# Two heads at once in row tiles of the array, compact keys, and new orders of work, in a fused four-layer transformer block

## The chip, the cores and the metric

One core of one Trainium2 chip runs the whole program in one launch. The metric is the device time in microseconds (us); lower is better.

## The reference, cut to what matters

The input is 32 sequences of 256 tokens with 128 features. Each sequence goes through four blocks: attention, feed-forward, rotary causal attention, and a block of two layers of local attention with a gated feed-forward each.

```python
x = x + attention16(layernorm(x))          # 16 heads of 8, scores / sqrt(128), all 256 keys
x = x + relu(layernorm(x) @ w1 + b1) @ w2 + b2           # width 512
x = x + attention16_rope_causal(layernorm(x)) @ wo.T     # 16 heads of 8, rotary, causal mask
x = x + ffn(layernorm(x))                  # two layers, each:
    # q, k, v = shift(x) @ wqkv : 8 heads of 64, l2 norm, rotary with scale
    # softmax(q k) over a window of 64 and the one before it, then @ wo, residual
    # shift, layernorm with gain and bias, @ w1, a * gelu(g), @ w2, residual
```

All of it is float32.

## The kernel before, in words

**Streams and units.** The work on a sequence is cut into four streams: ATTN0 (first attention and first feed-forward), ATTN1 (rotary attention), LOCAL0 and LOCAL1 (the two local layers). A stream is a list of units, each a small job that every engine knows (the unit `maxes` is, for TensorE, a matmul into a PSUM bank, and for VectorE the maximum over that bank). A bank is handed over by two semaphores of its own, one for filled and one for emptied. Every stream has one set of buffers, so it works on one sequence at a time, in order; the four streams work on four or five different sequences at once.

**Orders.** In which order an engine takes the units of the four streams is written out by hand in strings: `TURNS["tensor"]` and so on, one digit for the stream of the next unit, and `BANKS` gives the bank of each unit in TensorE's order. The strings describe one round of 216 units, one sequence of each stream. `plan()` plays the round 37 times: stream k takes up sequence n in round n + `TAKES_UP[k]` (0, 2, 3, 4), and its units from number `BEGINS[k]` on are a round later. So 27 rounds are full (rounds 5 to 31), and the five at either end are the same round with the units left out whose sequence is below 0 or above 31.

**Scores of the 16-head attentions.** A head has 8 features, and to keep float32 accuracy in the faster fp32r matmul each number is split in a high and a low part and the head's maximum is put in too: 32 rows of the contraction for a head, four heads to the 128 rows. `qT` holds four heads' queries on 128 partitions. `kT` before is wide: for each of the 16 heads a 128 x 256 block that is zero outside the head's 32 partitions, so a full-height matmul of `qT` (four heads) and the block gives one head's scores. ScalarE copies the transposed keys to `kS`, and SyncE's queue spreads them by four DMAs (L483) into `kT`; the unit `maxes` waits for them (`k_in`). `maxes` (L971; L975/L976 and L980/L982 with the causal mask as a matmul with the identity) makes 512 columns for a unit: two heads of 256 keys, or four of 128. VectorE takes the maxima (L802). `scores` (L992) makes the transposed scores, two matmuls of 256 queries for each unit; ScalarE takes the exponential (L656), GpSimd zeroes the causal part (L546). `mix` (L1011) multiplies the values with these, four heads at once, each in 32 columns of the array.

**Scores of the local attention.** A head has 64 features, so a pair of heads fills the 128 partitions. `kT2` is wide in the same way: two blocks for each pair, half zero, written by two half-height ACTIVATEs for each unit (L642). `scores2` is a mask matmul (L1071, L1079) and, in plain float32, L1073 or L1080; VectorE takes the maxima (L878), ScalarE the exponentials (L689). A plain float32 matmul is two instructions in the trace, an fp32r one is one. `mix2` (L1103) uses 64 columns of the array for each of two heads.

Of the kernel before, what the change touches and what calls it, by code (L numbers as in the profile page):

```python
# [8 lines left out]
STREAMS = 4  # L9
P = 128  # L10
# [17 lines left out]
def shape_constants():  # L28
# [23 lines left out]
    def table(c, s):  # L52
# [15 lines left out]
TAKES_UP = (0, 2, 3, 4)  # L68
BEGINS = (21, 33, 25, 8)


TURNS = {
    "tensor": (
        "20002220223311111333333222220002222222000022103333"
        "33333211100100333331000001130102222001233303303230"
        "02333331111133122000032220012220222222221111333330"
        "00330011311110011331011013333331112222222110100010"
        "0022200010111103"
    ),
    "scalar": (  # L80
        "22222332111333331312222000000022222222000033333333"
        "31111100000333330000031111222222200000333333222333"
        "33311111112200000002220012222221111333333322222300"
        "00330000033303333331111111111111112222222111122211"
        "1110000000000003"
    ),
    "vector": (
        "20020220232233303333321222222223333222221111133333"
        "32333111110000000000002113200000311130000011002233"
        "33320133302333301133222222213000003202223333220001"  # L90
        "11111222223111111111122133333223330000000000000000"
        "1111111111122223"
    ),
    "gpsimd": (
        "33333311333311133111112222222222222222222222211111"
        "11100000000000000000000000000000001112222222220000"
        "02212333333333333333333333333333302233333322222222"
        "22223333333111111111111111111111111111133000000000"
        "0000000000022222"
    ),  # L100
    "sync": (
        "22222222222222222222220000000000000000000000000000"
        "00333333333333333333333333333333333333333111111111"
        "11111111111111111000000000000000333333330000000000"
        "00111111111111111111111111222222222222222222222222"
        "2222222233333333"
    ),
}
BANKS = (
    "43672516420547631207624071245604751324605716750132"  # L110
    "76350263510674130746305207463123643750612562741532"
    "75432061757547342106714026751206732573014270641236"
    "5170236041725360"
# [20 lines left out]
def attention_units(rotary):  # L134
# [4 lines left out]
    units += [Unit("turn_k", u, bank=1, k_in=4 * 16 * u) for u in range(2)]  # L139
    units += [Unit("maxes", u, bank=1) for u in range(12 if rotary else 16)]  # L140
    units += [Unit("negmax", m_hi=1, m_ready=1)]
    units += [Unit("turn_q", u, source="with maxima", bank=1) for u in range(2)]
    for g in range(GROUPS):
        units += [Unit("scores", 4 * g + n, bank=1, **(dict(masked=1) if rotary else {})) for n in range(2 * TT)]
        units += [Unit("mix", g, bank=1)]
# [4 lines left out]
def local_units(last):  # L150
# [21 lines left out]
    units += [Unit("scores2", u, bank=1, max_done=1) for u in (0, 2, 3, 1, 4, 5)]  # L172
# [21 lines left out]
def stream_units(k):  # L194
# [11 lines left out]
    for n, u in enumerate(units):  # L206
        u.stream, u.number = k, n
        u.stage = TAKES_UP[k] + (1 if n >= BEGINS[k] > 0 else 0)
# [3 lines left out]
def merged_units(engine):  # L212

    queues = []
    for k in range(STREAMS):
        units = stream_units(k)
        queues.append(iter(units[BEGINS[k]:] + units[:BEGINS[k]]))
    return [next(queues[int(k)]) for k in TURNS[engine]]


def plan():

    last = max(u.stage for k in range(STREAMS) for u in stream_units(k))
    sequences = [{} for n in range(BATCH)]
    rounds, count = [], {}
    for now in range(BATCH + last):
        banks = iter(BANKS)
        units = merged_units("tensor")
        for u in units:
            u.buffers = [int(next(banks)) for i in range(u.uses)]  # L230
            u.sequence = now - u.stage
# [933 lines left out]
```

## Time and profile before

| | |
|---|---|
| median of 3 runs | 3203.81 us (3203.06 to 3206.26) |
| the profiled execution | 3203.11 us, of which the span of the trace is 3201.4 us |
| TensorE, matmuls (PE) | 2938.8 us busy, 92% |
| TensorE, weight loads (PEld) | 2173.0 us, 68% |
| VectorE (DVE) | 2391.8 us, 75% |
| ScalarE (ACT) | 2236.8 us, 70% |
| GpSimd (POOL) | 1561.3 us, 49% |
| granted TensorE clock, mean | 0.972 |

An engine's busy time is the union of its instructions. A matmul's record is longer than the time that it keeps the array: the next one starts before it ends. What a matmul costs in a row of them is read from start to start.

### The profile page before, as it was taken

To read this page: it belongs to the slowest core of one execution; us is meant where nothing else is said; L and a number is where in the kernel's file an instruction comes from. 1 tells how busy PE (TensorE), PEld (TensorE's weight loads), DVE (VectorE), ACT (ScalarE), POOL (GpSimd) and SP (SyncE) were. 2 spreads that over 40 slices of the span, in tenths; PEclk is the share of its full clock that TensorE was granted. 3 is DMA by queue.
4 is the path that set the end of the run, shared out by engine and by line. 5 is a ranking of instruction groups with operands and counts; after the bars stand their busy time and mean duration, and the time that the engine had idled before them with its cause. 6 is when DMAs were issued, how large, how long until landed. Compare 5 with 4: busy or idle time off the path is not lost.

```text
span 3201.4 us, 60855 instructions
## 1 busy us (share of the span) xinstructions
PE 2938.8 (92%) x20480; PEld 2173.0 (68%) x20480; DVE 2391.8 (75%) x6018; ACT 2236.8 (70%) x6084; POOL 1561.3 (49%) x1741
## 2 busy tenths in 40 slices
PE   4678999999999999999999999999999999999865
PEld 2456777777777777777777777777777777776643
DVE  4367778788777887887778778777787887776653
ACT  2346777777777777777777777777777777776643
POOL 1034445555455455545445555554455555545542
PEclk8789999999999999999999999999999999999987
DMA  2010000000000000000000000000000000000000
GB/s 72 15 22 17 11 13 19 18 18 19 19 11 19 13 17 19 19 19 19 11 13 18 18 19 19 20 18 12 13 17 19 19 19 19 11 12 10 11 4 5
DMA packets 78821, 55.03 MB, mean 17 GB/s; under 512 B 25226, under 2 KB 77876, under 8 KB 78516
## 3 DMA queue, kind: packets, MB, share of 16 engines
q1 hardware_dynamic: 78516, 51.12, 7.0%
q8 instruction: 172, 2.82, 0.4%
q14 instruction: 133, 1.09, 0.1%
HBM read 9.17 MB, written 4.19 MB: 4 GB/s over the span
## 4 chain that ended last, share of the span: by engine, by line
PE 60%; DVE 19%; ACT 8%; POOL 5%; issue 3%; DMA 2%; SPq 1%; DVEq 0%; POOLq 0%; ACTq 0%
PE bank L992 7%; PE bank L1011 7%; DVE negmax L802 5%; PE bank L1103 5%; PE bank L1080 5%; PE bank L1119 4%; PE bank L1047 4%; PE bank L1073 3%; PE bank L971 3%; DVE ss L844 3%; POOL rn L579 3%; ACT kT L642 2%; PE bank L1090 2%; PE bank L1058 2%; PE bank L956 2%
## 5 line engine op out<-in xcount | busy, mean ns | idle before, releaser
L802 DVE TENSOR_REDUCE negmax<-bank 128x2 f32<-128x512 f32 (+1 forms) x896 | 552.7, 678 | 31.2 <-PE bank L971 28.8
L656 ACT ACTIVATE probs<-bank 128x512 f32<-128x512 f32 (+1 forms) x1024 | 497.0, 571 | 44.3 <-PE bank L992 37.7
L579 POOL TENSOR_TENSOR rn<-ss,minus_half 128x16 f32<-128x16 f32 x128 | 372.7, 2912 | 150.4 <-DVE ss L859 150.0
L526 POOL TENSOR_TENSOR veps<-moments,eps_tile 128x2 f32<-128x2 f32 x192 | 37.8, 197 | 738.3 <-DVE moments L750 738.3
L546 POOL TENSOR_SCALAR_AFFINE_SELECT probs<-probs 128x256 f32<-128x256 f32 x512 | 210.9, 438 | 349.3 <-ACT probs L656 345.9
L1047 PE MATMUL bank<-wqkv_sb,hS 128*128 128x512 f32 x768 | 374.5, 605 | 6.1 <-ACT hS L611 4.5
L992 PE MATMUL bank<-qT,kT 128*128 128x256 f32 x2048 | 335.9, 297 | 19.3 <-ACT qT L633 7.6
L878 DVE TENSOR_REDUCE negmax<-bank 128x2 f32<-128x384 f32 (+1 forms) x384 | 230.2, 599 | 140.5 <-PE bank L1073 113.7
L992 PEld LDWEIGHTS bank<-qT,kT 128*128 128x128 f32 x2048 | 274.7, 191 | 69.2 <-issue 31.5
L633 ACT ACTIVATE qT<-bank 128x512 fp32r<-128x512 f32 x256 | 143.3, 629 | 151.8 <-PE bank L956 151.7
L567 POOL TENSOR_TENSOR rawA<-rawA,rope_sb 128x512 f32<-128x512 f32 x128 | 176.1, 1376 | 148.1 <-ACT rawA L675 148.1
L1011 PE MATMUL bank<-probs,V 128*16 128x256 f32 (+1 forms) x4096 | 237.4, 357 | 7.2 <-ACT probs L656 6.7
L689 ACT ACTIVATE P<-bank,negmax 128x192 f32<-128x192 f32 x512 | 215.4, 445 | 34.6 <-DVE negmax L878 28.5
L1119 PE MATMUL bank<-rawQ,w_sb 128*128 128x256 f32 (+1 forms) x768 | 214.4, 414 | 21.6 <-ACT rawQ L603 21.6
L567 POOL TENSOR_TENSOR rawB<-rawB,rope_sb 128x512 f32<-128x512 f32 x128 | 170.1, 1329 | 113.1 <-ACT rawB L675 113.1
L689 ACT ACTIVATE rawP<-bank,negmax 128x128 f32<-128x128 f32 x512 | 182.5, 381 | 43.2 <-DVE negmax L878 43.2
L971 PE MATMUL bank<-kT,qT 128*128 128x512 f32 x512 | 190.6, 455 | 22.0 <-DMA kT<-rawC 15.2
L1047 PEld LDWEIGHTS bank<-wqkv_sb,hS 128*128 128x128 f32 x768 | 132.9, 191 | 113.3 <-issue 81.4
L1080 PE MATMUL bank<-kT,rawQ 128*128 128x384 f32 x512 | 208.4, 488 | 0.0
L1011 PEld LDWEIGHTS bank<-probs,V 128*16 128x16 f32 x4096 | 97.4, 96 | 143.3 <-issue 82.6
L672 ACT ACTIVATE P<-bank 128x512 f32<-128x512 f32 x256 | 154.9, 605 | 56.4 <-PE bank L1047 55.2
L844 DVE TENSOR_REDUCE ss<-P 128x8 f32<-128x512 f32 x256 | 173.5, 678 | 26.4 <-ACT P L672 26.4
(149 smaller groups left out, 7839.6 us busy)
## 6 DMA issues: line engine op xcount, KB each, us to landing
kT<-rawC SPq DMA_DIRECT2D x256, 128.0 KB, 2.6
xin<-x SPq DMA_DIRECT2D x32, 128.0 KB, 2.1
out<-xout SPq DMA_DIRECT2D x32, 128.0 KB, 2.2
V<-YB SPq DMA_DIRECT2D x64, 63.5 KB
wqkv_sb<-wqkv SPq DMA_DIRECT2D x1, 1536.0 KB
V<-YB SPq DMA_DIRECT2D x64, 0.2 KB
w_sb<-w SPq DMA_DIRECT2D x1, 682.0 KB
w_sb<-w SPq DMA_DIRECT2D x2, 256.0 KB
```

What stands on the lines that cost most here:

```text
L567: nc.gpsimd.tensor_tensor(raw, raw, tab, ALU.mult).then_inc(sig("cos_part", u), 1)
L579: nc.gpsimd.tensor_tensor(rn[:, l, t].rearrange("p m h -> p (m h)"), ss[:, l, t].rearrange("p m h -> p (m h)"), minus_half[:], ALU.pow).th ...
L656: nc.scalar.activation(dst, src, ACT.Exp, scale=SCALE0 if k == ATTN0 else SCALE1)\
L689: last = nc.scalar.activation(dst, src, ACT.Exp, bias=negmax[:, k, t, hd:hd + 1], accum_out=expsum[:, l, t, hd:hd + 1])
L802: nc.vector.reduce_max(negmax[:, k, t, h0:h0 + nh], tile(u)[:, :].rearrange("p (h k) -> p h k", h=nh), AX.X, negate=True).then_inc(has_emp ...
L844: nc.vector.reduce_sum(ss[:, l, t, m, :], squares[m][:, l], AX.X).then_inc(sig("sums", u), 1)
L971: last = mm(bank, qT[:, k, g, t * P:(t + 1) * P], kT[:, k, 4 * g + 2 * e:4 * g + 2 * e + 2, :], start=True, stop=True)
L992: last = mm(tile(u)[:, i * SEQ:(i + 1) * SEQ], kT[:, k, 4 * g + 2 * e + i, t * P:(t + 1) * P], qT[:, k, g, :], start=True, stop=True)
L1011: last = mm(tile(u)[32 * n:32 * n + 16, q0:SEQ], V[:, k, t, 4 * g + n, :], probs[k][t][:, n * w:(n + 1) * w], start=t == 0, stop=t == 1)
L1047: mm(tile(u)[:], hS[:, l, t * P:(t + 1) * P], wqkv2_sb[:, l, m * INNER:(m + 1) * INNER], start=True, stop=True).then_inc(has_filled(u), 1)
L1080: last = mm(two, qT2[:, l, pr, P:SEQ], kT2[:, l, pr, :, WINDOW:SEQ], start=False, stop=True)
L1119: last = mm(tile(u)[0:n, half * SEQ:(half + 1) * SEQ], w1_2_sb[:, l, half * HID + at:half * HID + at + n], hT[k], start=True, stop=True)
```

## The change

- **Row tiles.** The scores of both 16-head attentions are matmuls of 32 rows (partitions 32n to 32n+31 hold head n of four), those of the local attention of 64 rows. A unit now holds two heads (`e` = 0, 1) that lie in different rows of the array and write two different banks, in turn: `bank=2`. `tile(u, e)`, `has_filled(u, e)` and so on name the bank. A round's number of units falls from 216 to 180.
- **The same numbers, a little fewer columns.** The matmuls of `maxes` are 256 (or 128) columns wide instead of 512. ATTN1's `scores` leave out the half of the second key tile's queries that the mask zeroes anyway. The masks stay full-height matmuls.
- **Compact keys.** `kT` is as `qT`, `kT2` as `qT2`: ScalarE copies a whole bank in one ACTIVATE for each unit. The four DMAs, `k_in`, `kS`, the zeroed blocks and the memsets at the start go.
- **mix** of ATTN0 waits for all of the group's probabilities before its first matmul, where it waited for those of each key tile.
- **Orders.** `FIRST` (339 units, ATTN0 4 sequences and 10 units, ATTN1 88 units, LOCAL0 72, LOCAL1 5), then 27 times `TURNS` (180 units) and `LAST` (561 units: 31, 92, 183 and 255 of the four streams), each with its banks. `TAKES_UP` and `BEGINS` go.

```diff
-    units += [Unit("turn_k", u, bank=1, k_in=4 * 16 * u) for u in range(2)]
-    units += [Unit("maxes", u, bank=1) for u in range(12 if rotary else 16)]
+    units += [Unit("turn_k", u, bank=1) for u in range(2)]
+    units += [Unit("maxes", u, bank=2) for u in range(6 if rotary else 8)]
...
-    units += [Unit("scores2", u, bank=1, max_done=1) for u in (0, 2, 3, 1, 4, 5)]
+    units += [Unit("scores2", u, bank=2, max_done=2) for u in range(3)]
...
+        return [next(queues[int(k)]) for k in FIRST[engine] + ROUNDS * TURNS[engine] + LAST[engine]]
...
-        kT = sb("kT", [P, 2, H16, SEQ], f32r)
+        kT = sb("kT", [P, 2, GROUPS, SEQ], f32r)
...
-                    for n in range(4):
-                        q = slice(32 * n, 32 * n + 32)
-                        sp.dma_start(heads[q, n], kS[q, k].rearrange("p u (g q) -> p (u g) q", g=2)).then_inc(sig("k_in", u), 16)
...
# maxes
-                        last = mm(bank, qT[:, k, g, t * P:(t + 1) * P], kT[:, k, 4 * g + 2 * e:4 * g + 2 * e + 2, :],
-                                  start=True, stop=True)
+                    for i in range(many):
+                        for e in range(2):
+                            rows = slice(32 * (2 * pair + e), 32 * (2 * pair + e) + 32)
+                            last = mm(tile(u, e)[:, i * keys:(i + 1) * keys], qT[rows, k, first + i, t * P:(t + 1) * P],
+                                      kT[rows, k, first + i, 0:keys], start=not whole and i == 0, stop=True, skip_group_check=True)
...
# scores
+                    for t in range(TT):
+                        q0 = P if k == ATTN1 and t == 1 else 0
+                        for e in range(2):
+                            rows = slice(32 * (2 * pair + e), 32 * (2 * pair + e) + 32)
+                            last = mm(tile(u, e)[:, t * SEQ:t * SEQ + SEQ - q0], kT[rows, k, g, t * P:(t + 1) * P],
+                                      qT[rows, k, g, q0:SEQ], start=True, stop=True, skip_group_check=True)
...
# scores2
+                    for i, pr in enumerate(pairs):
+                        for e in range(2):
+                            half = slice(HD * e, HD * e + HD)
+                            last = mm(parts[e][:, i, :], qT2[half, l, pr, queries], kT2[half, l, pr, keys],
+                                      start=False, stop=pr == pairs[-1], skip_group_check=True)
```

## Rows read from the trace of the kernel before

**Rows 1.** The page, busy time of each engine with its share of the span.
```profile
PE 2938.8 (92%) x20480; PEld 2173.0 (68%) x20480; DVE 2391.8 (75%) x6018; ACT 2236.8 (70%) x6084; POOL 1561.3 (49%) x1741
```

**Rows 2.** Windows: the first five rounds, 27 full ones, the last five.
```profile
core 0: us, PE busy (x) PEld busy (x) DVE busy (x) ACT busy (x) POOL busy (x), PEclk, DMA share, GB/s
0.00:412.00 412.00, 305.62 (x1932) 213.46 (x1933) 243.63 (x618) 200.13 (x498) 127.81 (x163) 0.89 0.11 28
412.00:2900.00 2488.00, 2414.39 (x17252) 1803.61 (x17251) 1987.77 (x5035) 1874.68 (x5117) 1306.56 (x1456) 1.00 0.07 17
2900.00:3201.40 301.40, 218.74 (x1300) 155.92 (x1298) 160.41 (x368) 162.01 (x471) 126.92 (x123) 0.89 0.02 6
```

**Rows 3.** Timeline (start us, length us), TensorE: `down0` of sequences 4 and 31.
```profile
384.14 0.38 PE L1040 MATMUL bank<-w_sb,rawC 128*128 128x128 f32 x2
...
2872.83 0.38 PE L1040 MATMUL bank<-w_sb,rawC 128*128 128x128 f32 x2
```

**Rows 4.** Groups by line and form, TensorE: the matmuls that the change touches.
```profile
L992 PE MATMUL bank<-qT,kT 128*128 128x256 f32 x2048 | 335.9, 297 | 19.3 <-ACT qT L633 7.6 <-issue 3.9 <-ACT P L689 0.6
L1080 PE MATMUL bank<-kT,rawQ 128*128 128x384 f32 x512 | 208.4, 488 | 0.0
L971 PE MATMUL bank<-kT,qT 128*128 128x512 f32 x512 | 190.6, 455 | 22.0 <-DMA kT<-rawC 15.2 <-DVE negmax L802 6.3 <-ACT probs L656 0.5
L1073 PE MATMUL bank<-kT,rawQ 128*128 128x256 f32 x512 | 132.3, 381 | 0.0
L980 PE MATMUL bank<-kT,qT 128*128 128x512 f32 x256 | 107.3, 437 | 1.9 <-DVE negmax L802 1.9
```

**Rows 5.** Timeline, TensorE, around a `mix` in a full round.
```profile
1522.55 0.84 PE L1011 MATMUL bank<-probs,V 128*16 128x256 f32 x16
1523.32 0.50 PE L971 MATMUL bank<-kT,qT 128*128 128x512 f32 x1
1523.66 1.11 PE L992 MATMUL bank<-qT,kT 128*128 128x256 f32 x8
1524.62 0.39 PE L971 MATMUL bank<-kT,qT 128*128 128x512 f32 x1
1524.84 0.39 PE L1071 MATMUL bank<-masks,ident_r 128*128 128x512 f32 x1
```

**Rows 6.** Timeline, TensorE: eight plain float32 matmuls, then around a `mix2`.
```profile
1500.11 1.89 PE L1119 MATMUL bank<-rawQ,w_sb 128*128 128x256 f32 x8
1501.84 0.81 PE L939 MATMUL bank<-wqkv_sb,probs 128*128 128x384 f32 x2
...
1537.92 0.27 PE L1092 MATMUL bank<-ident_r,P 128*128 128x128 f32 x1
1538.12 0.77 PE L1103 MATMUL bank<-rawA,V 128*64 128x192 f32 x8
1538.82 0.33 PE L1090 MATMUL bank<-ident_r,rawP 128*128 128x128 f32 x1
1538.98 0.27 PE L1091 MATMUL bank<-ident_r,P 128*128 128x128 f32 x1
```

**Rows 7.** Groups by line and form: maxima, and the copies of local keys.
```profile
L802 DVE TENSOR_REDUCE negmax<-bank 128x2 f32<-128x512 f32 x768 | 473.7, 678 | 29.8 <-PE bank L971 28.8
...
L642 ACT ACTIVATE kT<-bank 64x512 f32<-64x512 f32 x256 | 151.0, 590 | 5.3 <-PE bank L1058 2.2
```

**Rows 8.** Timeline, ATTN0 alone: two residuals, and between them the keys.
```profile
73.06 0.42 DVE L829 TENSOR_TENSOR probs<-xin,probs 128x256 f32<-128x256 f32 x1
...
94.82 1.29 ACT L637 ACTIVATE rawC<-bank 128x512 fp32r<-128x512 f32 x2 [0.26 <-PE bank L956]
96.21 2.53 SPq L483 DMA_DIRECT2D kT<-rawC  x4
100.69 4.67 PE L971 MATMUL bank<-kT,qT 128*128 128x512 f32 x10 [5.22 <-DMA kT<-rawC]
...
131.38 0.43 DVE L829 TENSOR_TENSOR probs<-xin,probs 128x256 f32<-128x256 f32 x1
```

**Rows 9.** Timeline, GpSimd: `finish` of sequences 26, 30 and 31.
```profile
2802.00 0.73 POOL L585 TENSOR_TENSOR xout<-XB,YB 128x256 f32<-128x256 f32 x1
...
3133.68 0.72 POOL L585 TENSOR_TENSOR xout<-XB,YB 128x256 f32<-128x256 f32 x1 [7.70 <-DVE YB L839]
...
3198.34 0.72 POOL L585 TENSOR_TENSOR xout<-XB,YB 128x256 f32<-128x256 f32 x1 [7.89 <-DVE YB L839]
```

More of the change, by code:

```diff
@@ L143, in attention_units @@
     for g in range(GROUPS):
-        units += [Unit("scores", 4 * g + n, bank=1, **(dict(masked=1) if rotary else {})) for n in range(2 * TT)]
+        units += [Unit("scores", 2 * g + n, bank=2, **(dict(masked=2) if rotary else {})) for n in range(2)]
         units += [Unit("mix", g, bank=1)]
@@ new lines, in max_part, with order @@
+def max_part(k, part):
+    if k == ATTN1 and part < 2:
+        return 0, 0, GROUPS, part
+    n = part + 2 if k == ATTN1 else part
+    return n // 4, 2 * (n // 2 % 2), 2, n % 2
+def plan():
+    sequences = [{(u.stream, u.number): u for k in range(STREAMS) for u in stream_units(k)} for n in range(BATCH)]
+    for n, units in enumerate(sequences):
+        for u in units.values():
+            u.sequence = n
+    def order(engine):
+        queues = [iter([u for units in sequences for (stream, n), u in units.items() if stream == k]) for k in range(STREAMS)]
+        return [next(queues[int(k)]) for k in FIRST[engine] + ROUNDS * TURNS[engine] + LAST[engine]]
+    orders = {engine: order(engine) for engine in TURNS}
+    banks, count = iter(FIRST_BANKS + ROUNDS * BANKS + LAST_BANKS), {}
+    for u in orders["tensor"]:
+        u.at = dict(count)
+        u.buffers = []
+        for i in range(u.uses):
+            b = int(next(banks))
+            count["bank", b] = count.get(("bank", b), 0) + 1
+            u.buffers.append((b, count["bank", b]))
+        for name, n in u.raises.items():
+            count[name, u.stream] = count.get((name, u.stream), 0) + n
+    return orders, sequences
@@ L354, in fused_block @@
         psum = [pb(f"bank{b}", [P, 512]) for b in range(NBANKS)]
-        rounds, sequences = plan()
+        orders, sequences = plan()
         rises = {}
@@ L427, in run @@
         def run(engine, unit):
-            for units in rounds:
-                for u in units[engine]:
-                    unit(u)
+            for u in orders[engine]:
+                unit(u)
         block = ctx.enter_context(nc.Block())
@@ L500, in fused_block @@
         ALL_LOADED = 16 * N_LOADS[0]
-        PRESETS, CLEARED = 9, NBANKS + 2
+        PRESETS, CLEARED = 9, NBANKS
         @block.gpsimd
@@ L985, in unit @@
+                    if k == ATTN1 and t == 1:
+                        for e in range(2):
+                            mm(tile(u, e)[:].rearrange("p (a k) -> p a k", a=2)[:, :, P:SEQ], ident_r[:],
+                               causal.unsqueeze(1).broadcast_to([P, 2, P]), start=False, stop=True, skip_group_check=True)\
+                                .then_inc(has_filled(u, e), 1)
                 elif u.kind == "scores":
-                    g, t, e = u.part // 4, u.part % 4 // 2, u.part % 2
+                    g, pair = u.part // 2, u.part % 2
@@ L1081, in unit @@
-                    last.then_inc(has_filled(u), 1)
+                        parts = [tile(u, e)[:].rearrange("p (a k) -> p a k", a=PAIRS) for e in range(2)]
+                        mask, queries, keys, pairs = band0, slice(0, P), slice(0, P), range(PAIRS)
+                    else:
+                        parts = [tile(u, e)[:].rearrange("p (a k) -> p a k", a=2)[:, :, 0:SEQ - WINDOW] for e in range(2)]
+                        mask, queries, keys, pairs = band1, slice(P, SEQ), slice(WINDOW, SEQ), range(2 * n - 2, 2 * n)
```

385 lines of the change are left out of this document (195 added, 190 removed).

## The prediction, made before the changed kernel was run

> **What bounds the kernel now.** I read the page's busy times first [rows 1]: TensorE is at 92% of the span, VectorE at 75%, ScalarE at 70%. An average over stages says little, so next come the windows [rows 2]. In the 27 full rounds TensorE's matmuls are busy 2414.4 of 2488.0 us, 97%, at a granted clock of 1.00; the other engines are far from it (VectorE 73.6 us a round, ScalarE 69.4, GpSimd 48.4). A round is (2872.83 - 384.14) / 27 = 92.2 us [rows 3], 89.4 us of it busy TensorE. So a round's length is TensorE's, and a microsecond off it is worth 27. The ends are another matter: 412 + 301.4 = 713 us for the work of five sequences, TensorE busy 524 us, clock 0.89. There a stream's own chain sets the pace.
>
> The sum starts from 27 x 92.2 + 713 = 3201.4, the span; 1.7 us lie outside it (3203.1, 0.7 below the median of the runs).
>
> **What a matmul costs.** Starts tell it. Eight fp32r matmuls of 256 columns take 1524.62 - 1523.66 = 0.96 us, 0.12 each; one of 512 is followed after 0.22 [rows 5], and I take 0.23. A plain float32 instruction of 256 columns takes (1501.84 - 1500.11) / 8 = 0.216, one of 128 0.11 by proportion, one of 384 0.32 [rows 6].
>
> **Do tiles of the array run at once?** The rows have no row tile, but they have column tiles. `mix` is 16 instructions in 4 tiles, 8 of 256 and 8 of 128 columns: one after another they would take 8 x 0.216 + 8 x 0.11 = 2.6 us, and the next matmul starts 0.77 us later [rows 5]. Four tiles run together, and their weight loads with them. `mix2`, two tiles, 8 instructions, 0.70 us instead of 4 x 0.16 + 4 x 0.11 = 1.08 [rows 6]. I take row tiles to behave alike: two heads in the time of one.
>
> **What that takes off a round.** Instructions of [rows 4] divided by 32:
> - ATTN0 `maxes`: 16 x 0.23 = 3.7 us, after it 32 of 256 columns in 16 slots of 0.12 = 1.9: -1.8.
> - ATTN0 `scores`: 32 x 0.12 = 3.8, after it 16 slots: -1.9.
> - ATTN1 `scores`: 3.8, after it 8 slots of 0.12 and 8 of 128 columns. A tile of 128 columns still loads 128 columns of weights, so I take 0.11 for those: 1.8, -2.0.
> - ATTN1 `maxes`: 12 x 0.23 = 2.8 (masks unchanged), after it 8 slots of 128 columns at 0.11 and 8 of 0.12: -0.9.
> - Local: 16 x 0.216 (L1073) + 16 x 0.32 (L1080) = 8.6, after it half: -4.3.
>
> Together -10.9 us. Bounds: nothing, if two row tiles don't run at once; and more, if two neighbouring units in different rows (11 places in TensorE's new string) run four heads at once as `mix` does: 11 x 0.24 = 2.6 more. I take 1.0 of it, since each unit waits for banks first. So -11.9.
>
> **What it adds: changes of tile shape.** Around `mix2`, from the start of L1092 at 1537.92 to that of L1091 at 1538.98 there are 1.06 us [rows 6]; two transposes (0.11 each) and the eight matmuls run two by two (2 x 0.16 + 2 x 0.11 = 0.54) account for 0.76. Going into the tiles and out of them costs 0.30, 0.15 a time. Out of `mix` it is more: the last L1011 work would end 4 slots (0.65) after 1522.55 but the next start is 0.77 later, and then L971 holds 0.34 where 0.23 is its own [rows 5]: 0.12 + 0.11 = 0.23. I read it as a drain of about 0.1 plus the incoming load that nothing hides: 0.01 for 16 columns of weights, 0.05 for 64 or a transpose, 0.11 for 128. Counting shapes along TensorE's string (32-row, 64-row, 32-column, 64-column tiles, full): 23 changes a round before, 61 after. Before: 6 x 0.11 + 6 x 0.15 + 11 x 0.17 = 3.4 us. After: 23 into row tiles x 0.20, 8 into `mix` x 0.11, 6 into `mix2` x 0.15, 24 to full x 0.18 = 10.7. Added: +7.3 us. Most of the gain goes back here. Bounds: 38 x 0.11 = 4.2 and 38 x 0.23 = 8.7.
> The Trainium skill ("TensorEngine Tiling (Array Packing)", Tiling Modes, key properties) says that changing the tiling mode drains the engine while other tiles of the same mode run and load in parallel; the trace agrees with both (0.15 to 0.23 us a change, 0.77 for 2.6 us of matmuls). By that page alone, which has no price for the drain, only the speedup would be counted and a round would be near 81 us.
>
> **The other engines.** VectorE's reductions are as many and as wide (L802 678 ns each [rows 7]): 73.6 us a round stay. ScalarE loses half of its key copies: 8 x 0.59 a round become 4 of about 0.62 [rows 7], 4.7 to 2.5, -2.2, hidden in a full round. SyncE's four DMAs a sequence and attention go; in full rounds TensorE waits for little but its own queue, so that is worth nothing there. What was hidden behind TensorE gets less cover: VectorE 73.6 of 88 instead of 92, and a unit holds two of eight banks. I add 0.4 us of waits.
>
> A round: 92.2 - 11.9 + 7.3 + 0.4 = 88.0. 27 x 88.0 = 2376, -112 against 2488. Ends of this term: 84 (four at once, cheap changes) and 99.7 (no overlap: 92.2 + 7.3, + 0.2 for split matmuls).
>
> **The ends.** They have strings of their own now, a unit moved to where it is ready.
> - *Start.* ATTN0 alone takes 131.38 - 73.06 = 58.3 us for a sequence [rows 8]. The keys' way through the DMAs goes from 96.11 (end of L637) to 100.69: without it 4.5 us less. Maxima are VectorE's pace there and exponentials ScalarE's, so faster matmuls give little; the mix that waits for both key tiles takes a little back. FIRST is four whole ATTN0 sequences and 10 units: first residual at 73.1 - 4.5 = 68.6, three more at 57 (53.8 alone, the other streams come in) = 239.6, and from a residual to the first maxima 100.69 - 73.06 - 4.5 = 23: 263 us. Between 245 and 300.
> - *End.* LAST holds 4.9 of LOCAL1's sequences. Before, five took 3198.34 - 2802.00 = 396.3 us, the last, alone, 64.7 [rows 9]. Alone it loses 1.2 us of key copies. Two interleaved chains with TensorE freer: 78 + 72 + 66 + 64 + 63 = 343, less 8 for the tenth of a sequence already done, and 3 for the store: 338. Between 310 and 375.
>
> Ends: 263 + 338 = 601, -112. In all 2376 + 601 + 1.7 = **2979 us**.
>
> **The rivals.**
> 1. *Row tiles don't run at once* (the other side; here the change would not do what it says). One mechanism: the loads of two row tiles, 128 columns each, follow each other. For it: `mix` loads only 16 columns a tile, so the rows don't show two full-width loads together. Against: sixteen such loads fit into the 0.77 us of [rows 5], and those of 64 columns in `mix2` go in pairs too. Then a round is 99.7 us, 27 x 99.7 = 2692, ends about 645: 3340. It turns slower when less than about 3 of the 10.9 us come. Chance 0.11.
> 2. *Consumers bind.* A `maxes` unit fills two banks in 0.24 us that VectorE empties in 1.36; with 73.6 of 88 us busy its queue is late more often, and TensorE stands for a bank with two needed at once. The Trainium skill names this ("TensorEngine Tiling (Array Packing)", PSUM Bottleneck). Price: 3 us of waits a round, or changes at their upper bound: 91 x 27 = 2457, ends 620: 3079. Against: before, VectorE had 18 us free a round. Chance 0.20.
> 3. *More overlap.* Four heads at once at all 11 places and changes of 0.11: a round 84, ends 570: 2268 + 572 = 2840. For it: `mix` does four. Chance 0.17.
> 4. *Nothing*: 0.02. Gains and changes would have to cancel to 0.2% of the time, which is about what this kernel's measurement can tell.
>
> **The numbers.** Forecast 0.50, its own range 2915 to 3045 (round 86 to 90, ends 555 to 655 not both at once). The range for 8 in 10 takes in rivals 2 and 3 and leaves out rival 1 and the far edge of 3: 2840 to 3130. Faster 0.87 (the forecast, 2, 3), same 0.02, slower 0.11.
>
> **What would show each step.** Right: matmuls of `maxes` and `scores` that start in pairs, a few ns apart, and the next pair 0.12 us later; pairs of local matmuls 0.11 and 0.16 us apart; gaps of 0.2 us at a change of shape; a round near 88 us; the first full round from 263 us and the last 338 us after the 27; no wait for keys. Wrong: paired starts 0.12 apart (rival 1), TensorE waiting for L802, L656 or L689 inside rounds (rival 2), quartets (rival 3). The forecast is most exposed in the price of 38 added changes, which row tiles may share or escape, and in the ends, which I size from lone chains.

## The result, and the profile after

The changed kernel takes 3123.61 us (median of 4, 3116.41 to 3130.85), before on the same chip 3203.43: a ratio of 0.975, 95% interval 0.9725 to 0.9775. It is 80 us faster where I forecast 224. The time lies inside the stated range, and outside the forecast's own one of 2915 to 3045.

The profiled execution took 3130.85 us, its span is 3128.7. First the page's busy times of the changed kernel, to be laid beside [rows 1]:

```profile
PE 2816.9 (90%) x22656; PEld 1976.8 (63%) x22656; DVE 2411.2 (77%) x6016; ACT 2147.9 (69%) x5956; POOL 1548.2 (49%) x1741
```

TensorE lost 122 us, and the span only 73: what it no longer works, it partly waits. Then the windows of the changed kernel: the strings `FIRST`, 27 times `TURNS`, `LAST`, and two single rounds.

```profile
core 0: us, PE busy (x) PEld busy (x) DVE busy (x) ACT busy (x) POOL busy (x), PEclk, DMA share, GB/s
0.00:303.00 303.00, 198.32 (x1415) 127.18 (x1415) 151.98 (x421) 125.11 (x300) 75.42 (x107) 0.79 0.06 20
303.00:2751.50 2448.50, 2322.10 (x19118) 1645.79 (x19117) 2027.53 (x5049) 1803.99 (x5022) 1294.60 (x1458) 0.98 0.02 6
2751.50:3128.70 377.20, 296.50 (x2128) 203.80 (x2126) 231.67 (x548) 218.77 (x636) 178.21 (x178) 0.91 0.02 5
1184.30:1273.90 89.60, 84.88 (x709) 60.07 (x708) 75.00 (x188) 66.61 (x186) 47.95 (x54) 1.00 0.02 6
1366.20:1458.50 92.30, 87.75 (x710) 62.30 (x709) 75.26 (x188) 67.05 (x186) 48.03 (x54) 0.96 0.02 6
```

A round is 2448.5 / 27 = 90.7 us (92.2 before, 88.0 forecast). In a round at full clock TensorE is busy 84.9 us, as the sum had it (89.4 - 11.9 + 7.3 = 84.8), and that round lasts 89.6: 4.7 us idle, where the sum had 3.2. Half of the rounds are longer, up to 92.3, at a mean clock below 1.00: on average another 1.1 us a round. `FIRST` takes 303 us (forecast 263), `LAST` 377 (338).

How the tiles run is seen in the timeline of TensorE, at a place like that of [rows 5]. The first fence is a whole stretch, the second the first 50 ns of its line L1030 (weight loads).

```profile
1603.99 1.06 PE L1050 MATMUL bank<-probs,V 128*16 128x256 f32 x16
1604.97 0.51 PE L1030 MATMUL bank<-qT,kT 32*128 32x256 f32 x8
1605.42 0.73 PE L1113 MATMUL bank<-masks,ident_r 128*128 128x512 f32 x2
1606.08 0.71 PE L1118 MATMUL bank<-kT,rawQ 64*128 64x128 f32 x8
```

```profile
1604.97 0.20 PEld L1030 LDWEIGHTS bank<-qT,kT 32*128 32x128 f32 x4 [0.42 <-issue]
```

Eight matmuls of 256 columns, two units of two heads, need 0.45 us to the next start, where eight of full height need 0.96 [rows 5]: four row tiles start together, their loads of 128 columns too. In the same stretch of the trace the next four loads start 0.11 us later and their matmuls 0.22 us after the first four; L1113 starts 0.20 us after those, where one such matmul is followed by its like after 0.12 in the run at full height below, so the change of shape takes the other 0.08. That the four DMAs are gone shows in the page: 21.76 MB moved instead of 55.03.

What TensorE waits for in the 27 rounds (engine, line waited for: us in all, times, longest), changed kernel:

```profile
PE bank L1030 <- ACT qT L687: 23.4, 27, 0.9
PE bank L975 <- DVE rawP L886: 21.0, 27, 0.8
PE bank L1030 <- ACT P L730: 19.7, 27, 0.7
PE bank L992 <- DVE KB L829: 15.2, 27, 0.6
PE bank L969 <- DVE negmax L836: 13.5, 27, 0.5
PE bank L1085 <- ACT P L730: 12.3, 27, 0.5
PE bank L1113 <- DVE negmax L836: 5.7, 18, 0.4
PE bank L1113 <- ACT probs L697: 3.3, 7, 0.5
```

The first six come once a round, each is under 1 us, and all are for VectorE or ScalarE. The local exponential L730 is released by VectorE's maxima, but that doesn't make each wait behind it VectorE's lateness. The chain that ends in one of them (L1030 behind P L730, 0.72 us) and VectorE's line at that place:

```profile
1517.65 0.70 DVE negmax L914
...
1518.38 2.90 ACT rawP L730 x16
1521.27 1.61 ACT P L730 x8
...
1523.15 0.81 ACT P L730 x4
...
1524.10 0.63 PE bank L1030 x6
...
1517.65 1.29 DVE L914 TENSOR_REDUCE negmax<-bank 128x4 f32<-128x512 f32 x2 [3.58 <-PE bank L1118]
```

VectorE had stood idle for 3.58 us, waiting for TensorE's scores. Its maximum takes 0.70 us, and then ScalarE works for 5.6 us before TensorE can go on: this wait is for the length of ScalarE's work. At the other place (L1085 behind P L730) VectorE comes to its maximum straight from maxima of L836, so there its work is in the chain too.

### The profile page after: what moved, and what is told of

It is laid out like the page before. It is cut to its first block, busy times and chain, and to the rows that moved or that the text cites. A ratio compares the mean times of both kernels' runs of the same rounds, so it can differ in the third digit from the quotient of the medians.

```text
span 3128.7 us, 65895 instructions
## 1 busy us (share of the span) xinstructions
PE 2816.9 (90%) x22656; PEld 1976.8 (63%) x22656; DVE 2411.2 (77%) x6016; ACT 2147.9 (69%) x5956; POOL 1548.2 (49%) x1741
## 2 busy tenths in 40 slices
DMA packets 41974, 21.76 MB, mean 7 GB/s; under 512 B 21131, under 2 KB 41013, under 8 KB 41653
## 4 chain that ended last, share of the span: by engine, by line
PE 43%; DVE 27%; ACT 19%; POOL 5%; issue 4%; DMA 0%; DVEq 0%; POOLq 0%; SPq 0%
DVE negmax L836 10%; ACT rawP L730 6%; ACT P L730 5%; PE bank L1050 5%; PE bank L1143 5%; PE bank L1151 4%; PE bank L1030 4%; PE bank L1096 3%; DVE ss L879 3%; PE bank L1159 3%; POOL rn L633 3%; PE bank L1130 2%; ACT probs L697 2%; PE bank L1085 2%; PE bank L1011 2%
## 5 line engine op out<-in xcount | busy, mean ns | idle before, releaser
L836 DVE TENSOR_REDUCE negmax<-bank 128x2 f32<-128x512 f32 (+1 forms) x896 | 554.4, 679 | 25.7 <-PE bank L1011 25.6
L1085 PE MATMUL bank<-wqkv_sb,hS 128*128 128x512 f32 x768 | 390.9, 625 | 30.9 <-ACT P L730 12.7
L914 DVE TENSOR_REDUCE negmax<-bank 128x2 f32<-128x384 f32 (+1 forms) x384 | 211.7, 593 | 135.1 <-PE bank L1118 133.4
L1050 PE MATMUL bank<-probs,V 128*16 128x256 f32 (+1 forms) x4096 | 259.5, 373 | 24.4 <-ACT probs L697 22.2
L1011 PE MATMUL bank<-kT,qT 32*128 32x256 f32 (+1 forms) x2048 | 216.8, 324 | 25.7 <-DVE negmax L836 16.1
L1085 PEld LDWEIGHTS bank<-wqkv_sb,hS 128*128 128x128 f32 x768 | 131.9, 193 | 163.3 <-issue 125.6
L730 ACT ACTIVATE rawP<-bank,negmax 128x128 f32<-128x128 f32 x512 | 179.7, 376 | 79.7 <-DVE negmax L914 79.7
L1011 PEld LDWEIGHTS bank<-kT,qT 32*128 32x128 f32 x2048 | 143.9, 191 | 133.3 <-issue 105.1
L1030 PE MATMUL bank<-qT,kT 32*128 32x256 f32 (+1 forms) x2048 | 180.3, 323 | 49.5 <-ACT qT L687 24.7
L1030 PEld LDWEIGHTS bank<-qT,kT 32*128 32x128 f32 x2048 | 126.9, 194 | 135.2 <-issue 76.3
L730 ACT ACTIVATE P<-bank,negmax 128x192 f32<-128x192 f32 x512 | 211.0, 470 | 0.1
L1159 PE MATMUL bank<-rawQ,w_sb 128*128 128x256 f32 (+1 forms) x768 | 195.5, 393 | 3.3 <-ACT rawQ L657 3.3
L1118 PE MATMUL bank<-kT,rawQ 64*128 64x128 f32 (+1 forms) x2048 | 192.2, 317 | 0.0
L902 DVE TENSOR_TENSOR rawA<-rawA,rn 128x512 f32<-128x512 f32 x128 | 151.7, 1185 | 49.6 <-POOL rawA L628 49.6
```

The source lines that it names most:

```text
L730: last = nc.scalar.activation(dst, src, ACT.Exp, bias=negmax[:, k, t, hd:hd + 1], accum_out=expsum[:, l, t, hd:hd + 1])
L836: nc.vector.reduce_max(negmax[:, k, t, head:head + 4 * many - 3:4], tile(u, e)[:, :].rearrange("p (h k) -> p h k", h=many), AX.X, negate=T ...
L1011: last = mm(tile(u, e)[:, i * keys:(i + 1) * keys], qT[rows, k, first + i, t * P:(t + 1) * P], kT[rows, k, first + i, 0:keys], start=not w ...
L1030: last = mm(tile(u, e)[:, t * SEQ:t * SEQ + SEQ - q0], kT[rows, k, g, t * P:(t + 1) * P], qT[rows, k, g, q0:SEQ], start=True, stop=True, s ...
L1050: last = mm(tile(u)[32 * n:32 * n + 16, q0:SEQ], V[:, k, t, 4 * g + n, :], part, start=t == 0, stop=t == 1)
L1085: mm(tile(u)[:], hS[:, l, t * P:(t + 1) * P], wqkv2_sb[:, l, m * INNER:(m + 1) * INNER], start=True, stop=True).then_inc(has_filled(u), 1)
```

## The experiments

The theory after the result (A): the tiles overlap as forecast, and the gain is lost because VectorE, with as much to do as before, is late in the fixed orders. Against it: the changes of shape cost more than the sum had (B); the overlap is incomplete, or the new orders and the missing DMAs bring part of the gain (C); the clock takes it (D). In the table "round" is the mean of the 27, "idle" the part of it without TensorE, "low" the time at the clock of 1.2 GHz in `FIRST` / the rounds / `LAST`, all from the profiled execution. "Row tiles" are the change; each other row is the changed kernel with one edit.

| kernel | time, us | ratio, 95% interval | `FIRST` | round | idle | `LAST` | low |
|---|---|---|---|---|---|---|---|
| row tiles | 3123.6 | 0.975 [0.9725, 0.9775] | 303.0 | 90.7 | 4.7 | 377.2 | 126 / 75 / 66 |
| full height | 3200.1 | 0.9993 [0.9983, 1.0003] | 292.0 | 93.4 | 3.1 | 380.4 | 41 / 0 / 49 |
| both heads in the same rows | 3325.2 | 1.0388 [1.0372, 1.0403] | 322.4 | 96.4 | 2.7 | 398.8 | 147 / 65 / 83 |
| tiles in local attention only | 3163.1 | 0.9873 [0.9859, 0.9888] | 301.3 | 92.2 | 4.2 | 375.6 | 72 / 0 / 52 |
| tiles in 16-head attention only | 3177.4 | 0.992 [0.9905, 0.9934] | 303.9 | 92.3 | 3.6 | 383.0 | 123 / 99 / 69 |
| mix by pair | 3115.1 | 0.973 [0.9712, 0.9748] | 294.1 | 90.7 | 4.7 | 378.3 | 58 / 68 / 69 |
| more matmuls at the start | 3118.8 | 0.9739 [0.9724, 0.9753] | 304.9 | 90.3 | 4.7 | 371.4 | 65 / 41 / 56 |
| short maxima | 3024.2 | 0.944 [0.9426, 0.9454] | 290.3 | 87.4 | 3.6 | 370.2 | 113 / 0 / 56 |
| fewer changes of shape | 3236.9 | 1.010 [1.0083, 1.0117] | 303.5 | 94.7 | 7.5 | 373.6 | 126 / 164 / 55 |
| 4 scalings on GpSimd | 3081.2 | 0.9614 [0.96, 0.9628] | 301.0 | 88.9 | 3.8 | 378.9 | 79 / 41 / 69 |
| 6 scalings on GpSimd | 3086.4 | 0.963 [0.9614, 0.9646] | 304.9 | 88.7 | 3.7 | 387.2 | 126 / 38 / 86 |
| 6 scalings, mix by pair | 3084.3 | 0.9623 [0.9608, 0.9637] | 303.3 | 88.8 | 3.7 | 383.1 | 123 / 48 / 75 |

**1. Full height.** No row tile is left; orders, banks and compact keys stay. The matmuls contract over all 128 rows of the compact keys, so the scores are those of several heads summed.

```diff
-                            rows = slice(32 * (2 * pair + e), 32 * (2 * pair + e) + 32)
+                            rows = slice(0, P)
...
-                            half = slice(HD * e, HD * e + HD)
+                            half = slice(0, P)
```

> The changed kernel with its own orders and banks, but all its score matmuls over the full 128 rows (each then sums the scores of four heads, or of two in the local attention, so its scores are not the reference's; sizes, banks and all other work are the same). No two heads run at once, and the 38 added changes of tile shape in a round are gone. Theory A (row tiles bring what was forecast, 11.9 us of TensorE a round for 7.3 of shape changes, and the miss lies in waits, in the clock and at the ends): TensorE 84.9 + 11.9 - 7.3 = 89.5 us busy a round, a round of 92 to 94, total 3165 to 3220. Theory B (the row tiles bring nothing net, the 80 us come from the orders and the missing key transfers): the total stays within 20 us of 3124.

Measured 3200.07 us, as before. New orders, units of two banks, and keys without DMA are by themselves worth nothing that can be measured: rounds 1.2 us longer, ends 41 us shorter (672 against 713). C falls in this part, and the row tiles carry the whole gain. (Of the 61 changes of shape in a round 28 are left here and 33 are gone, not 38: the new orders have five more than the old ones by themselves.) The windows of this kernel (columns as above; `FIRST`, then the rounds):

```profile
0.00:292.00 292.00, 197.39 (x1415) 145.50 (x1416) 152.91 (x421) 124.32 (x300) 75.55 (x107) 0.93 0.07 20
292.00:2813.20 2521.20, 2437.16 (x19118) 1949.95 (x19116) 2027.54 (x5049) 1809.27 (x5022) 1293.36 (x1457) 1.00 0.02 6
```

TensorE is busy 2437.2 / 27 = 90.3 us a round, 5.4 more than in a full-clock round with tiles, so the tiles take off 5.4 net of their changes of shape, and only 2.7 reach the round. Both kernels issue the same matmuls in the same order, so full-clock rounds of the two traces can be laid side by side, from start to next start, leaving out the ten places with a wait. Score matmuls followed by one of their own shape take 11.4 us less in a round with tiles. The new changes of shape, 31 of the 33, take 3.9 us more (0.13 each), and all other places 1.5 more. That is the sum's -11.9 and +7.3, nearly. VectorE works the same 2027.5 us. What TensorE waits for in the rounds, full height:

```profile
PE bank L1030 <- ACT qT L687: 26.2, 27, 1.0
PE bank L975 <- DVE rawP L886: 21.3, 27, 0.8
PE bank L992 <- DVE KB L829: 15.1, 27, 0.6
PE bank L969 <- DVE negmax L836: 11.0, 27, 0.4
PE bank L1030 <- ACT P L730: 10.4, 27, 0.4
```

The difference to the list above is what the tiles gave back: L1030 and L1085 behind the local exponentials (+9.3, +12.3), L1113 behind VectorE's and ScalarE's release of its banks (+9.0), L969 (+2.5), less 2.8 at qT: some 30 of the 42 us that idle time grew by. Two thirds of these 30 stand behind ScalarE's local exponentials. The wait for rawP, 21 us (4.7 before the change), came with the orders.

**2. Both heads in the same rows.** All shapes and changes of shape stay, and the two heads of a unit can't run at once (the second head of a pair gets the first one's rows, so its scores are left out).

```diff
-                            rows = slice(32 * (2 * pair + e), 32 * (2 * pair + e) + 32)
+                            rows = slice(64 * pair, 64 * pair + 32)
...
-                            half = slice(HD * e, HD * e + HD)
+                            half = slice(0, HD)
```

> The changed kernel, but the two heads of a unit use the same rows of the array (both read the first one's queries and keys, so the second head's scores are wrong): same instructions, same tile shapes and changes, but no overlap inside a unit. Theory A: TensorE 84.9 + 11 to 12 us a round, a round of 98 to 101, total 3350 to 3430. Theory B (the overlap is worth little, or is eaten by other limits such as weight loads): less than 3250. Minus e1 it prices the 38 changes of shape: by A 38 x 0.19 = 7.3 us a round, some 200 us in all.

3325 us, near rival 1's 3340: had the tiles not overlapped, the change would have been 4% slower. Two 32-row units side by side still overlap here, in different pairs of rows; eight L1030 take 0.67 us to the next start, where four tiles at once took 0.45 and full height takes 0.96. At full clock a round of this kernel is 95.3 us, 1.9 over full height's 93.4. Laid beside run 1 as above, the overlap left in it is worth 2.7 us a round, the new changes of shape cost 4.0, and all other places take 1.3 more. With the overlap whole it was 3.9 and 1.5: either way at most 5.4 us a round for the 33 changes, 0.16 each where the sum had 0.19. B falls.

**3 and 4. One kind of tile at a time.** `rows = slice(0, P)` alone (tiles in the local attention only), `half = slice(0, P)` alone (tiles in the 16-head attention only). What is at full height again gives summed scores, as in run 1.

> The changed kernel with row tiles in the local attention alone; the scores of the 16-head attentions are full-height (each sums four heads, so they are not the reference's). Against the kernel with all at full height (93.4 us a round, 3200 us) by the prediction's terms: 4.3 us less matmul time, 6 units a round with two changes of shape each, some +2.2 us: TensorE 88.2 busy, a round of 91 to 91.8, total 3135 to 3160. If changes cost much more than 0.2 us, nothing is left: 3190 to 3210.

> The changed kernel with row tiles in the 16-head attentions alone; the local scores are full-height (each sums two heads, so they are not the reference's). By the prediction's terms against all at full height: 7.6 us less matmul time, about 26 more changes of shape, +5 us: TensorE 87.7 us busy, a round of 91 to 92, total 3135 to 3170; so both halves would bring about the same, for twice as many changes here. The clock falls in the rounds here as in the changed kernel if 32-row matmuls are behind that, and doesn't in the run with local tiles only.

-1.2 and -1.1 us a round from full height's 93.4, and -2.7 together. They differ in the clock: with 64-row tiles alone the rounds have no stretch at 1.2 GHz, with 32-row tiles alone 99 us of them. In rounds at full clock the two take 92.2 and 90.8 us, -1.2 and -2.6, and both together 89.6, -3.8: so the halves add, and the 32-row tiles are worth twice the 64-row ones, with 24 changes of shape a round for 10.

They also part the idle time. It grows by 1.6 us a round over full height, and the local tiles alone bring 1.1 of that (4.2 against 3.1), the others alone 0.5 (3.6). TensorE's waits in the rounds with local tiles only:

```profile
PE bank L1030 <- ACT P L730: 19.7, 27, 0.7
PE bank L1085 <- ACT P L730: 11.2, 27, 0.4
PE bank L1113 <- DVE negmax L836: 9.2, 27, 0.3
```

Of the 30 us that are new against full height, 20 are behind ScalarE's exponentials of that very attention (L1030 10.4 there, L1085 none) and 9 behind VectorE: TensorE has the local scores ready sooner and then waits for the same exponentials.

**5. Short maxima.** VectorE's maxima of the 16-head attentions (L836) read the first half of each head's keys only; TensorE's work is unchanged.

```diff
-                                             tile(u, e)[:, :].rearrange("p (h k) -> p h k", h=many), AX.X, negate=True)\
+                                             tile(u, e)[:, :].rearrange("p (h k) -> p h k", h=many)[:, :, 0:256 // many], AX.X, negate=True)\
```

> The changed kernel, but VectorE takes the maxima of the 16-head attentions over the first half of each head's keys only (so the maxima are not those of the whole row): 28 reductions a round over 256 instead of 512 columns, about 0.25 us less each, 7 us of VectorE's 75 us a round. Theory A1 (part of the 4.7 us in which TensorE stands in a round is lateness of VectorE): a round of 87 to 88.5 us, total 3040 to 3085. Theory A2 (TensorE's own string and the length of the streams' chains set the waits, not how busy VectorE is): a round within 0.7 us of 90.7, total 3095 to 3125, the rest from the start and the end.

3024 us, 100 less than with whole maxima, from an edit to VectorE's work alone: the group is 415 ns instead of 679, which is 7 us a round, and the round falls by 3.3 to 87.4. This is the run that A needed for VectorE's part. The group in question, and TensorE's waits in the rounds:

```profile
L836 DVE TENSOR_REDUCE negmax<-bank 128x2 f32<-128x256 f32 (+1 forms) x758 | 273.3, 415 | 70.2 <-PE bank L1017 45.1 <-PE bank L1011 25.0
```

```profile
PE bank L1030 <- ACT qT L687: 23.4, 27, 0.9
PE bank L1030 <- ACT P L730: 19.7, 27, 0.7
PE bank L1085 <- ACT P L730: 16.7, 53, 0.5
...
PE bank L969 <- DVE negmax L836: 6.2, 27, 0.2
```

The wait for rawP is gone, that of L1113 for negmax too, L969 is halved. Those behind the local exponentials don't shrink (36.4 us, 32.0 before this edit), so what this run takes away is not what the tiles had added: it shows that the round hangs on VectorE's work as well, for the most part at a wait that full height has too. All 27 rounds are now at full clock and alike (87.3 to 87.5). Of the 3.3 us, 1.1 is the clock; of the other 2.2, half shows as less idle time and half as less busy time of the same instructions, which the records don't resolve further. `FIRST` falls by 13 us and `LAST` by 7.

**6. Fewer changes of shape.** Units of TensorE's string are moved next to others of their shape: 57 changes a round instead of 61.

```diff
-        "1110330102222111002022103333333332222221122222200022011102333333333000313113100013333332222000332203"
+        "1110301032222111002022103333333332222221122222200022101102333333333000313111300013333332222000332203"
```

> The changed kernel with three units moved in TensorE's string of the full round, with their banks (qkv2 of LOCAL1 behind the maxes and scores units that stand around it, mix of ATTN1 and turn of ATTN1 ahead of a row-tile unit): 57 changes of shape a round instead of 61, everything else the same. Theory A (a change costs TensorE 0.2 us and a round's length is TensorE's): 0.8 us less a round, 15 to 22 us in all, 3100 to 3108. Rival (the time comes back as waits of the moved units and of those behind them): 3115 to 3135.

A clear miss: 3237 us, 1% slower than before. Four changes less could save 0.8 us a round by the sum's price, and the round is 4.1 longer: 2.8 by idle time (7.5), the rest at the lower clock, since all 27 rounds now have a stretch at 1.2 GHz, 164 us in all, where 13 had one. New once-a-round waits stand in the trace behind VectorE (L1030 for negmax, 1.3 us each; L969 for the attention output, 1.1 each). The moved units had been the cover for a bank's way through VectorE. It speaks for hand-offs that bind (A) against B, though it doesn't price the changes.

**7. Mix by pair.** `mix` waits for one pair of heads, issues both its key tiles, then the other pair: the old wait's slack given back.

```diff
-                    if k == ATTN0:
-                        for sem, count in newest(*of("scores", 2 * g, 2 * g + 1)):
-                            pe.wait_ge(sem, count)
...
+                    for pair in range(2):
+                        if k == ATTN0:
+                            for sem, count in newest(*of("scores", 2 * g + pair)):
+                                pe.wait_ge(sem, count)
```

> The changed kernel, but mix waits for the probabilities of its first two heads, issues their matmuls of both key tiles, and only then waits for the other two heads. Theory A (at the start the whole-group wait lengthens ATTN0's chain: 4.9 us a group where it was 3.4): 1 us less a group there, 4 groups x 4 sequences = 10 to 16 us at the start, and up to 0.5 us a round of waits on ScalarE: 3095 to 3115. Rival: two tiles at once instead of four make the mix itself longer, 8 mixes a round by up to 0.4 us: 3150 to 3200.

`FIRST` is 9 us shorter, the rounds are unchanged. The stated time, 3115 against 3124, has an interval that overlaps the other's; the 9 us rest on one profile of each.

**8. More matmuls at the start.** Eight extra full-height matmuls into an unused half of the bank, ahead of the wait in ATTN0's `mix`, for the first four sequences.

```diff
+                    if k == ATTN0 and u.sequence < 4:
+                        for n in range(8):
+                            mm(tile(u)[:, SEQ:2 * SEQ], ident_r[:], masks[:, 0:SEQ], start=True, stop=True)
```

> The changed kernel with eight extra full-height matmuls of 256 columns, into unused columns of mix's own bank, before the wait for the probabilities in each mix of ATTN0's first four sequences. They sit where TensorE waits. Theory A (at the start the clock of 1.2 GHz sets the chain's length, granted 0.79 on average): the clock of the first 303 us rises, mix falls from 1.8 to about 0.9 us, 10 to 20 us less in all: 3104 to 3114. Rival (the chain there is ScalarE's and VectorE's, or the extra work is in its way): 0 to 15 us more.

The time at 1.2 GHz in `FIRST` falls from 126 to 65 us and `FIRST` stays (305 against 303): with more work in TensorE's waits the clock is higher there and the start no shorter. The extra matmuls are 14 us of work themselves (212.4 against 198.3 us busy), so D falls for the start unless they cost just what the clock gave back.

**9 to 11. Scalings on GpSimd.** If VectorE's lateness binds, moving work off it should pay. `scale2` of the local queries and keys (L902) is a multiply with a broadcast that GpSimd can do; GpSimd is busy 48 of 90 us a round.

```diff
+                elif u.kind == "scale2" and u.part < 2:
...
+                    rot = (q2, k2)[m][:, l, t, :].rearrange("p (h d) -> p h d", h=HEADS)
+                    nc.gpsimd.tensor_tensor(rot, rot, rn[:, l, t, m, :].unsqueeze(2).broadcast_to([P, HEADS, HD]), ALU.mult)\
+                        .then_inc(sig("rope_ready", u), 1)
...
-                elif u.kind == "scale2":
+                elif u.kind == "scale2" and not (u.part < 2):
```

> Four of the twelve scalings of a round's local query and key rows (scale2, parts 0 and 1 of both streams) are done by GpSimd instead of VectorE; nothing else changes. Each took VectorE about 1.05 us, so VectorE loses some 4 us of the 74 us that it works in a round of 90; GpSimd, busy 48 us a round, gains some 5. Theory A, VectorE's lateness is what a round waits for now (7 us less of it gave 3.3 us a round in the run with short maxima): a round of 88.5 to 90 us instead of 90.7, 3065 to 3105 us in all. Rival, a slower engine in the chain of the local block makes that chain late instead: a round of 90.7 or more, 3115 us or more.

> Six scalings a round (parts 0 to 2 of both streams) go to GpSimd: 6.3 us off VectorE, some 8 us onto GpSimd. Theory A: a round of 87.5 to 89.5 us, 3040 to 3095 us in all, below the run with four. Rival, GpSimd's string becomes late: at or above the run with four, 3115 us or more if it eats the whole gain.

> The edit of the run with six scalings on GpSimd, and the mix that waits for one pair of heads at a time. By what the mix by pair gave alone (9 us in the first round, nothing in the others) it should be 5 to 12 us below the run with six. If it is level with that run, the gain of the first round came from a cover that VectorE's shorter work gives already.

With four a round the kernel takes 3081.2 us, 42 below the changed kernel and the fastest of the kernels that leave nothing out: ratio 0.9614 to before. Its windows (the rounds) and its group on GpSimd:

```profile
301.00:2701.00 2400.00, 2297.93 (x19119) 1632.36 (x19118) 1959.12 (x4941) 1799.42 (x5022) 1406.21 (x1567) 0.99 0.02 6
```

```profile
L642 POOL TENSOR_TENSOR rawB<-rawB,rn 128x512 f32<-128x512 f32 x55 | 57.5, 1045 | 4.3
```

VectorE falls from 75.1 to 72.6 us a round (GpSimd takes 1.04 us for one, VectorE 1.22 or 0.73, by the buffer), the round from 90.7 to 88.9 (at full clock from 89.6 to 88.4, so 0.6 of the 1.8 us is the clock), and TensorE's wait for rawP, 21 us, is gone here too. The rival of these runs (GpSimd as the new late engine) didn't come true. Six a round bring nothing over four: the round is 0.2 us shorter, and the ends (692 us against 680) are longer; the intervals of the two overlap. With mix by pair the gain expected, 5 to 12 us, isn't there (3084.3 against 3086.4): `FIRST` is 303 against 305, so the 9 us of run 7 don't carry over, and whether they were real there stays open.

## Why the prediction was wrong, step by step

- **Row tiles run at once: right**, and with them two neighbouring units at four heads where they meet. Rival 1 falls by the paired starts, and run 2 gives its price (3325 against 3340 worked out, close in part because overlap between units is left in it). The Trainium skill ("TensorEngine Tiling (Array Packing)", Tiling Modes, key properties) says that tiles of a mode run and load in parallel; the starts above, four loads of 128 columns within 50 ns, agree.
- **What a round keeps TensorE busy: right as a sum**, 84.8 worked out, 84.9 measured at full clock. Its two terms hold within 2 us: run 1 has 11.4 off for 11.9, and 5.4 on for 7.3, for 33 changes of shape and not 38.
- **The step that failed in the rounds: "What was hidden behind TensorE gets less cover ... I add 0.4 us of waits."** Idle time was to be 3.2 us a round and is 4.7, some 43 us over 27 rounds. I had named the mechanism as rival 2, with its argument against: VectorE "had 18 us free a round". It fails twice. First, a mean of free time doesn't bound a wait in a fixed order: VectorE still has 15 us free in a round of 90.7, and taking 7 us (run 5) or 2.5 us (run 9) off it shortens the round by 3.3 and 1.8, of which 2.2 and 1.2 at full clock. Second, it looked at VectorE alone: two thirds of the waits that can be put down to the tiles stand behind ScalarE's local exponentials (runs 1, 3 and 5), 5.6 us in a row that TensorE now reaches sooner. The section PSUM Bottleneck of the Trainium skill's "TensorEngine Tiling (Array Packing)" says that a faster TensorE can leave the emptying of PSUM as the bottleneck; runs 1, 3 and 5 agree. That rival 2 put a round at 91 and it is 90.7 is in part luck: its 3 us of waits were 1.5, and the clock made up most of the rest.
- **A term the sum did not have: the clock**, 1.1 us a round, 30 in all. Before, the rounds were at 1.00 [rows 2], and I took that for granted. (Rounded: the 27 rounds of before have five short stretches at 1.2 GHz, 17 us in all, where the changed kernel has 75.)
- **The start, 303 for 263, is a term that was sized too small.** First residual at 72.9 us where I had 68.6 (+4.3); the next three after 59.2, 64.1 and 76.7 us where I had three of 57 (+29); from the fourth to the first full round 30.3 where I had 23 (+7). The keys did come earlier, the first maxima at 94.7 us instead of 100.7 [rows 8], and the chain behind them took it back. "The mix that waits for both key tiles takes a little back" shows in the timeline of the changed kernel:

```profile
111.66 1.91 PE L1050 MATMUL bank<-probs,V 128*16 128x256 f32 x16 [2.07 <-ACT probs L697]
113.50 1.49 PE L1030 MATMUL bank<-qT,kT 32*128 32x256 f32 x8
116.54 1.91 PE L1050 MATMUL bank<-probs,V 128*16 128x256 f32 x16 [1.55 <-ACT probs L697]
118.37 1.49 PE L1030 MATMUL bank<-qT,kT 32*128 32x256 f32 x8
```

  A group takes 118.37 - 113.50 = 4.87 us, `mix` after the exponentials and the next scores after it, with no overlap, and both at 1.2 GHz (1.91 against 0.84 in a round). Before, the half of `mix` for the first key tile ran while ScalarE was at the second, and a group took 122.22 - 118.80 = 3.42 us, so "a little" was 1.5 us of each of four groups in a sequence:

```profile
118.80 1.33 PE L992 MATMUL bank<-qT,kT 128*128 128x256 f32 x8
120.69 0.63 PE L1011 MATMUL bank<-probs,V 128*16 128x256 f32 x8 [0.56 <-ACT probs L656]
...
122.22 1.22 PE L992 MATMUL bank<-qT,kT 128*128 128x256 f32 x8
```

  Full height has 292 us here, mix by pair 294, short maxima 290: each takes some 10 of the 40. What the third and fourth sequence wait for, with the other streams running, I did not take apart.
- **The end, 377 for 338, too.** The intervals between the last residuals were to be 78, 72, 66, 64 and 63 us, less 8. Windows of the changed kernel between them:

```profile
2751.40:2840.90 89.50, 81.42 (x685) 56.85 (x682) 70.60 (x174) 61.73 (x173) 47.39 (x52) 0.98 0.02 4
2840.90:2915.10 74.20, 62.86 (x479) 44.24 (x477) 48.69 (x127) 50.83 (x149) 40.76 (x46) 0.98 0.02 5
2915.10:2999.90 84.80, 69.11 (x490) 45.08 (x489) 55.30 (x124) 49.56 (x144) 50.11 (x50) 0.92 0.02 4
2999.90:3063.30 63.40, 49.79 (x318) 36.01 (x316) 33.39 (x78) 34.68 (x109) 20.88 (x18) 0.89 0.02 5
3063.30:3125.70 62.40, 33.43 (x164) 21.64 (x164) 23.80 (x47) 22.08 (x62) 18.50 (x15) 0.75 0.01 4
```

  The lone chains (63.4, 62.4) were right. The first interval is still a full round, TensorE busy 81 of 89.5 us (+11.5), the third holds 69 us of TensorE (+19), and the 8 us for work already done were not there. I sized stages by a lone chain that hold three or four streams. Row tiles bring the ends nothing: 680 us with them, 672 at full height.

The account, against 2979: waits 43, clock 30, start 40, end 39, which is 152. The profiled execution is 3130.9, 152 above. So the larger half of the miss, 79 us, is in the ends, whose sizes came from lone chains, and no one step carries it. Only for the rounds do runs show what stood in the failed step's place; for the ends the record shows which stretches were too short, and not by experiment why. The time lies inside the stated range because the range took in rival 2 (3079).

**Open.** Why the clock falls in some dense rounds (below); what the waits behind the local exponentials (L730) would give back, since no run moved work off ScalarE or shortened it; the start's third and fourth sequence; an exact price of a change of shape.

## What to carry to other kernels

When the engine that bounds a stage gets faster, don't read the slack of the next ones from their mean free time: in a fixed order single hand-offs bind far earlier (here VectorE at 83% of the round), and so does a serial piece of work that the fast engine now reaches sooner (here 5.6 us of exponentials on ScalarE at 74%). Look at what the engine waited for did just before, since one that stood idle itself was not late. Measure by making that engine's work shorter, as in run 5, before hunting for more savings on the first; then move work to the engine that is truly idle. Stages at the ends are sized by the streams that run in them and not by a lone chain, and a tuned order is tied to the durations that it was tuned for (run 6).

## What was not expected of the hardware

- **Low clock inside dense rounds.** With 32-row tiles there were 75 us (all tiles) and 99 us (these alone) at 1.2 GHz inside the 27 rounds; in runs 1 (full height) and 3 (64-row tiles alone) none. But 32-row tiles are neither needed nor enough: the kernel before has 17 us in its rounds, in five stretches, and short maxima, with all tiles, have none. The windows around one such stretch of the changed kernel, the same place of a round in which it didn't come, and a low stretch of the kernel before (last line; TensorE had waited 1.11 and 0.66 us in the 2 us ahead of it):

```profile
1294.90:1301.70 6.80, 5.93 (x35) 3.27 (x35) 6.77 (x16) 6.25 (x12) 3.76 (x5) 1.00 0.08 23
1301.70:1308.50 6.80, 6.76 (x50) 5.13 (x51) 4.45 (x10) 4.24 (x8) 3.91 (x4) 0.50 0.00 0
...
1204.90:1211.70 6.80, 5.93 (x35) 3.40 (x35) 6.76 (x16) 6.61 (x12) 3.42 (x5) 1.00 0.07 19
...
852.90:856.30 3.40, 3.40 (x10) 2.67 (x11) 3.40 (x5) 1.07 (x3) 3.40 (x4) 0.51 0.73 154
```

  Ahead of the fall TensorE was busy 5.93 of 6.8 us with one wait of 0.87 (L1030 for qT), and in the clean round it was busy just as long. Short maxima keep that wait (0.9) and have no low stretch. What decides isn't settled.
- **Four 32-row tiles load and multiply at once** with 128 columns of weights each (four starts within 50 ns, the next four loads 0.11 us later and their matmuls 0.22), which the column tiles of before, with 16 columns each, couldn't show.
- **GpSimd came near VectorE** on the broadcast multiply of 128 x 512 (1.04 us; on VectorE 1.22 for rawA and 0.73 for rawB). The Trainium skill ("GPSIMD Engine Reference", Performance versus the Vector engine) puts two-input elementwise work at about twice VectorE's time; for this broadcast operand the trace doesn't agree: 1.4 times rawB's time, and less than rawA's.
